# Edge tiles that belong to one node tile each, in a two-layer graph network

## The reference, cut to what matters

```python
h = relu(layernorm(x));  hh = (h @ W.T).reshape(N, 4, 32)
a_src, a_dst = (hh * att_src).sum(-1), (hh * att_dst).sum(-1)
alpha = leaky_relu(a_src[src] + a_dst[dst], 0.2)
ex = exp(alpha - segment_max(alpha, dst)[dst])
w = ex / segment_sum(ex, dst)[dst]
x = x + segment_sum(hh[src] * w[:, :, None], dst) + bias
h = relu(layernorm(x))
m = relu(concat(h[src], h[dst], edge_attr) @ W1 + b1) @ W2 + b2
x = x + segment_sum(m, src)
```

## Time and profile before

| | us |
|---|---|
| median of 3 runs (7310.71 to 7337.83) | 7331.83 |
| span of the profiled execution, first to last instruction | 7415.3 |
| start, up to the first batch's sums | 178 |
| attention stage, 62 batches | 2970 |
| node stage | 97 |
| target stage, 62 batches | 2800 |
| source stage and output | 1370 |

### The profile page before, as it was taken

One profiled execution on the slowest core, in us unless ns is written; L12 is line 12 of the kernel. 1 busy time (PEld: TensorE's weight loads), 2 busy tenths in 40 slices (PEclk: granted clock), 3 DMA queues, 4 the chain that ended last, 5 costly groups with the idle time before them and its releaser, 6 DMA issues.

```text
span 7415.3 us, 158159 instructions
## 1 busy us (share of the span) xinstructions
PE 5830.3 (79%) x34498; PEld 4483.9 (60%) x34499; DVE 4072.9 (55%) x14406; ACT 2876.8 (39%) x8241; POOL 3921.0 (53%) x3713
## 2 busy tenths in 40 slices
PE   4777776777777767767788788778778779999999
PEld 3666665666566656645555555555555557777777
DVE  5555555555555555653333333343333358888887
ACT  3333333333333333322222222222222247777776
POOL 4555555555555555465555555555555555555543
PEclk6777777766767776779988888898888889999999
DMA  3311111111111111366666666666666669999998
GB/s 89 123 37 37 37 37 37 37 36 37 37 37 37 37 37 37 102 191 194 193 194 190 195 189 194 190 192 190 197 185 188 191 178 214 214 214 213 214 212 195
DMA packets 860289, 993.31 MB, mean 134 GB/s; under 512 B 307992, under 2 KB 663224, under 8 KB 859774
## 3 DMA queue, kind: packets, MB, share of 16 engines
q1 hardware_dynamic: 662494, 608.23, 31.0%
q0 software_dynamic: 190592, 378.22, 19.3%
q10 hardware_dynamic: 6816, 3.38, 0.2%
HBM read 726.65 MB, written 262.76 MB: 133 GB/s over the span
## 4 chain that ended last, share of the span: by engine, by line
PE 66%; another core or an unknown queue 12%; issue 10%; DVE 6%; DVEq 3%; ACT 2%; DMA 1%; ACTq 0%; POOL 0%; SPq 0%; POOLq 0%
PE bank L1527 16%; PE bank L1686 10%; PE bank L1621 9%; PE bank L1619 8%; PE bank L1676 6%; PE bank L1455 4%; PE bank L1465 4%; PE bank L1609 2%; DVEq L246 2%; ACT arena L623 1%; PE bank L1574 1%; PE bank L1667 1%; DVE arena L1193 1%; DVE arena L1238 1%
## 5 line engine op out<-in xcount | busy, mean ns | idle before, releaser
L494 POOL DMA_INDIRECT arena<-h_tab,arena x1612 | 1592.0, 988 | 1474.2 <-PE bank L1527 857.6
L544 POOL DMA_INDIRECT xr<-arena x1612 | 1585.0, 983 | 1233.2 <-ACT arena L705 731.7
L1527 PE MATMUL bank<-arena 128*128 128x136 f32 x6448 | 1625.0, 392 | 77.6 <-DVE arena L1044 6.2
L1621 PE MATMUL bank<-arena 128*128 128x256 f32 x3224 | 1111.9, 430 | 486.4 <-DVE arena L1254 359.7
L705 ACT ACTIVATE arena<-bank 128x256 f32<-128x256 f32 x1612 | 598.0, 384 | 2141.4 <-PE bank L1621 1246.7
L1527 PEld LDWEIGHTS bank<-arena 128*128 128x128 f32 x6448 | 1227.4, 263 | 149.2 <-issue 108.6
L623 ACT ACTIVATE arena<-bank 128x256 bf16<-128x256 bf16 x1612 | 614.4, 383 | 1803.5 <-PE bank L1455 1108.3
L1044 DVE TENSOR_TENSOR arena<-arena,bank 128x272 f32 x1612 | 699.9, 434 | 1006.3 <-PE bank L1527 689.8
L1619 PE MATMUL bank<-arena 128*128 128x256 f32 x3224 | 1113.0, 430 | 9.9 <-DVE arena L1238 9.9
L1621 PEld LDWEIGHTS bank<-arena 128*128 128x128 f32 x3224 | 655.6, 212 | 707.7 <-DVE arena L1254 450.2
L558 POOL DMA_INDIRECT arena<-p_tab,arena x428 | 667.9, 1561 | 659.6 <-DMA arena<-p_tab,arena 439.6
(11 more groups left out here) (253 smaller groups left out, 7124.2 us busy)
## 6 DMA issues: line engine op xcount, KB each, us to landing
arena<-xr SPq DMA_DIRECT2D x428, 516.0 KB
arena<-q_tab SPq DMA_DIRECT2D x1612, 128.0 KB
arena<-in_edge_attr SPq DMA_DIRECT2D x61, 832.0 KB
arena<-rel_tab SPq DMA_DIRECT2D x124, 224.0 KB
arena<-h_tab,arena POOLq DMA_INDIRECT x1612
xr<-arena POOLq DMA_INDIRECT x1612
arena<-rel_tab SPq DMA_DIRECT2D x124, 192.0 KB
xr<-arena SPq DMA_DIRECT2D x26, 516.0 KB
```

Of the source, the lines that this page charges most:

```text
L494: pool.indirect_dma_start(G[:, q, t, :], None, h_tab, bass.IndirectOffsetOnAxis(ap=idx[:, q, t:t + 1], axis=0)).then_inc(sem(f"gath{q}"), 16)
L544: pool.indirect_dma_start(xr, bass.IndirectOffsetOnAxis(ap=pos[:, q, t:t + 1], axis=0), Rb[:, t, :], None).then_inc(sem(f"scat{m}"), 16)
L1527: last = pe.matmul(PSB[3 + t % 2][:, k * H * MW:(k + 1) * H * MW], OH[:, (t + 2 * q) % 4, k * P:(k + 1) * P], flat(msg[:, t, :, :]), start ...
L1621: pe.matmul(o, EAT[:, (t // 2 + q) % 2, :], w1z[:, t % 2, :], start=False, stop=True).then_inc(sem("main_done"), 1)
```

## The change

An edge tile now belongs to one node tile only. The row of 128 edges that straddles a border is taken twice, once for each node tile, with the edges of the other node tile masked (source and target -1). So T = 13 x 128 = 1664 tiles (1612 rows, at most 48 of them twice, the rest empty), and NB = 64 batches.

- One-hot, its transpose and its float form are 128 wide; there is one transpose, one expand matmul, one aggregation matmul (136 columns) and one add of 136 columns for a tile.
- At the start, ScalarE loads the last target of each row of edges (4 bytes each); DVE and TensorE count rows below each border, and from that the bin and the row of each tile (whole_rows, tile_rows). The bins go through DRAM (bt_tab) into bin_row. GpSimd gathers the rows of targets and sources with 27 indirect DMAs. DVE masks them (target_rows, source_rows) and makes the flags before they are transposed (flag_rows); ScalarE moves the flags out of PSUM. The tables d0_tab and col_tab and their loads go.
- In the target stage the window of q_tab starts at 128 times the bin. The edge features of a batch are loaded tile by tile: 26 DMAs of 32 KB in the place of one of 832 KB, each with its row (tile number less bin) worked out in registers, after a second load of 26 bins.
- Masked edges go to rows of xr of their own (dump is 26 wide).

```diff
-BT = 26
-NG = T // TG
+BT = 26
+NG = 13
+T = NG * P
 NB = T // BT
...
-        G, OHb = X([2, BT, GW]), X([2, BT, 2 * P], BF16)
+        G, OHb = X([2, BT, GW]), X([2, BT, P], BF16)
...
+            def load_ea(b, q, last=False):
+                regs = bins(ENG.SP, b, BT)
+                whole = TAIL - (NB - 1) * BT if last else BT
+                for t in range(whole):
+                    row = nc.s_assert_within(b * BT + t - regs[t], 0, WHOLE - 1, ...)
+                    sp.dma_start(EAb[:, q, t, :], ea[bass.ds(row * P, P), :]).then_inc(sem(f"ea_in{q}"), 16)
...
-                    regs = nc.values_load_multi_w_load_instructions(d0row[0:1, bass.ds(b * RB, BT)], engines=[ENG.SP], ...)
+                regs = bins(ENG.SP, b, BT)
...
-                        sp.dma_start(Qw[:, t, :], q_tab[bass.ds(regs[t], P), :]).then_inc(sem(f"rows_in{m}"), 16)
+                        sp.dma_start(Qw[:, t, :], q_tab[bass.ds(regs[t] * P, P), :]).then_inc(sem(f"rows_in{m}"), 16)
...
-            pool.wait_ge(sem("e_in"), 16 * 15)
-            for a in range(3):
-                M.tensor_copy(rF[:, a, :], rI[:, a, :]).then_inc(sem("rF_ready"), 1)
+            pool.wait_ge(sem("tiles_ready"), 1)
+            for v, into, n, landed in ((dst, rD, NG + 1, "rD_in"), (src, rS, NG, "rS_in")):
+                for j in range(n):
+                    pool.indirect_dma_start(into[0:p, j, :], None, wholes(v), bass.IndirectOffsetOnAxis(ap=trowI[0:p, j:j + 1], axis=0)).then_inc(sem(landed), 16)
...
+            def target_rows():
+                dve.wait_ge(sem("rD_in"), 16 * (NG + 1))
+                link(V.tensor_tensor(r3, rD, tbase.unsqueeze(2).to_broadcast([P, NG + 1, P]), ALU.subtract))
+                link(V.tensor_scalar(valid, rel, 0.0, None, ALU.is_ge))
+                link(V.scalar_tensor_tensor(valid, rel, float(P), valid, ALU.is_lt, ALU.mult))
+                link(V.scalar_tensor_tensor(rel, rel, 1.0, valid, ALU.add, ALU.mult))
...
-                A.activation(ohT[:, t % 2, :], PSB[t % 2][:].bitcast(BF16)[:, 0:2 * P], ACT.Copy)
+                A.activation(ohT[:, t % 2, :], PSB[t % 2][:].bitcast(BF16)[:, 0:P], ACT.Copy)
...
-                a = flat(acc[:, bass.ds(regs[t], 2), :])
-                V.tensor_tensor(a, a, PSB[3 + t % 2][:, 0:2 * H * MW], ALU.add)
+                a = flat(acc[:, bass.ds(regs[t], 1), :])
+                V.tensor_tensor(a, a, PSB[3 + t % 2][:, 0:H * MW], ALU.add)
...
-                for k in range(2):
-                    last = pe.transpose(PSB[t % 2][:].bitcast(BF16)[:, k * P:(k + 1) * P], OHb[:, s, t, k * P:(k + 1) * P], identb)
+                pe.transpose(PSB[t % 2][:].bitcast(BF16)[:, 0:P], OHb[:, s, t, :], identb)
...
-                for k in range(2):
-                    last = pe.matmul(ab_ps[half][:, j, :, :]..., ohT[:, t % 2, k * P:(k + 1) * P], flat(aT3[:, bass.ds(regs[t] + k, 1), :, :]), start=(k == 0), stop=(k == 1))
+                pe.matmul(ab_ps[half][:, j, :, :]..., ohT[:, t % 2, :], flat(aT3[:, bass.ds(regs[t], 1), :, :]), start=True, stop=True)
...
-                    for k in range(2):
-                        last = pe.matmul(PSB[3 + t % 2][:, k * H * MW:(k + 1) * H * MW], OH[:, (t + 2 * q) % 4, k * P:(k + 1) * P], flat(msg[:, t, :, :]), start=True, stop=True)
+                    pe.matmul(PSB[3 + t % 2][:, 0:H * MW], OH[:, (t + 2 * q) % 4, :], flat(msg[:, t, :, :]), start=True, stop=True)
```

More of the change, by code:

```diff
@@ L231, in flat @@
             return v.rearrange(f"p {d} -> p ({d})") if len(v.shape) > 2 else v
+        LISTS = [(j, min(j + 4, NG)) for j in range(0, NG, 4)]
+        FLAGS = [(0, 7), (7, NG)]
+        turned_tiles = lambda v: v[:, 0:T].rearrange("e (p j) -> e j p", j=NG)
         PIECES = [(m * BT // 4, (m + 1) * BT // 4) for m in range(4)]
@@ L360, in load_windows @@
                 B = b * BT
-                regs = nc.values_load_multi_w_load_instructions(
-                    d0row[0:1, bass.ds(b * RB, BT)], engines=[ENG.SP], min_val=0, max_val=NPAD,
-                    skip_runtime_bounds_check_because="the first target node of a tile")[1]
+                regs = bins(ENG.SP, b, BT)
                 for m, (lo, hi) in enumerate(PIECES):
@@ L816, in _, with whole_rows @@
             V.memset(srcE[:, T:], -1.0)
-            V.memset(dE[:, T:], -1.0)
-            V.memset(nE[:, T:], -1.0)
+            V.memset(dBE[:, T:], -1.0)
+            for v in (lastE, s1E, s2E):
+                V.memset(v[:, T:], 0.0)
+            def whole_rows():
+                dve.wait_ge(sem("w_in"), 80)
+                dve.wait_ge(sem("pads"), 4)
+                link(V.tensor_tensor(below, lastV.unsqueeze(1).to_broadcast([P, NT, NG]),
+                                     edge.unsqueeze(2).to_broadcast([P, NT, NG]), ALU.is_lt))
+                V.tensor_reduce(whole, below, AX.X, ALU.add).then_inc(sem("wx_ready"), 1)
@@ L855, in _ @@
                     if n == 1:
-                        dve.wait_ge(sem("w_in"), 48)
+                        dve.wait_ge(sem("w_in"), 80)
                         V.tensor_scalar(attb[:, 0:H], hm, att[:, 0:1], None, ALU.mult)
                         V.tensor_scalar(attb[:, H:], hm, att[:, 1:2], None, ALU.mult).then_inc(sem("wx_ready"), 1)
+                    if n == 2:
+                        tile_rows()
                     if n == 5:
-                        dve.wait_ge(sem("rF_ready"), 3)
-                        for g in range(NG):
-                            V.tensor_scalar(relB[:, g, :], rF[:, 1, g * P:(g + 1) * P], rF[:, 1, g * P:g * P + 1], None,
-                                            ALU.subtract).then_inc(sem("rF_ready"), 1)
+                        target_rows()
                     if n == 6:
-                        lists((0,))
+                        source_rows()
                     scaled(n - 1)
@@ L1135, in _ @@
                 hot(1, 1, t, True)
[L1136 removed]
+            empty_bins()
             logits(0, 0, 0)
@@ L1437, in _ @@
                     project(c - 1)
-            lists((1, 2))
-            project(NCH - 1)
-            lists(range(3, NG))
+                else:
+                    pe.wait_ge(sem("wx_ready"), 1)
+                    pe.matmul(PSB[3][:, 0:NT], ones, whole, start=True, stop=True).then_inc(sem("wx_ps"), 1)
+            pe.wait_ge(sem("row_made"), 1)
+            lists(srcR, 0)
+            project(NCH - 1)
+            lists(rel, 1)
+            pe.wait_ge(sem("hx_ready"), NCH)
+            for a, v in enumerate((lastR, firstR, finalR)):
+                pe.wait_ge(sem("row_made"), a + 2)
+                flags(v, a)
             pe.wait_ge(sem("hx_used"), NCH)
```

301 lines of the change are left out of this document (161 added, 140 removed).

## The result

The change made the kernel slower: 7465.9 us (median of 4 runs, 7462.9 to 7491.6) against 7334.8 us (4 runs) on the same chip, ratio 1.0192 with a 95% interval of 1.0168 to 1.0216. The forecast was 6744 us, with 0.04 for slower.

What follows compares the result with a forecast made beforehand. PE was taken as the longest member of the attention stage's ring of waits. Attention -696, target +90, start +10 and node +8 sum to -588 from 7415.3: span 6827, less 83.5 to the median, 6744 us; range 6558 to 7020.

Steps and rivals of the forecast that it cites:

- no batch can be shorter than 32.8: Attention stage: POOL's 26 gathers, starting every 1.26 us, set a floor of 32.8 us for a batch.
- rival 1: Attention stage: POOL's floor is reached, 32.8 to 34.5 us for a batch; at 33, 6558 us in all; chance 0.20.
- I take 36, between PE's and DVE's readings: Attention batch: PE's busy plus idle time gives 32.4 us, DVE's busy time plus waits 37.7; 36 taken, bounds 32.8 and 42.4.
- The term of 8 us: Attention stage: DVE's 8.0 us of waits in a batch that the profile calls remote or issue, assumed to stay.
- the ring: Attention stage: each batch is a ring of waits through PE, ACT, DVE and POOL, PE the longest member; 48.8 us.
- Rival 2: Attention stage: PE drops to its half clock and the stalls stay, 40 us for a batch, 6992 us in all; chance 0.20.
- Rival 4: Attention stage: order of waits holds the batch at 48.8 us, 7538 us in all; slower above 45.5; chance 0.05.
- So the move is hidden, with 5 us to spare: Target stage: SP's added transfers delay the next batch's first piece, but it still comes before it is needed at 45 us.
- SP's sum of 34 to 43, likely 38 us: Target stage: SP's time for a batch with 25 more DMAs, about 0.6 us each, and a second load of bins.
- rival 3: Target stage: SP becomes the bound at 1 us for an edge-feature DMA, batch 50 us, 7051 us in all; chance 0.08.
- The three signs that I had named for being wrong: POOL still waits long for PE each batch; window loads end DVE's or PE's target-stage waits; start grows over 25 us.
- Start, +10 forecast: Start: 27 gathers take 34 to 39 us, first h_tab gather 10 us later than 75.8; +10 us, bounds 0 and +25.

Runs made afterwards that it cites:

- e12: Changed kernel with a small GpSimd fill after each attention gather, gathers 1.44 us apart and more, late-signal chip: 7566.1 us, 1.0216 of before.
- e11: Kernel before the change, without GpSimd's gathers from the third batch on, late-signal chip: 6448.9 us, attention batch 33.3 us.
- e15: Changed kernel without GpSimd's gathers from the third batch on, late-signal chip: 6707.0 us, attention batch 30.7 us.
- e4: Changed kernel, a batch's edge features in one transfer, no second load of bins, chip without late signals: 5897.4 us, 1.0146 of before.
- e9: Changed kernel, edge features in 13 two-tile transfers from static rows, no second load of bins, late-signal chip: 7346.2 us, target batch 45.0 us.
- e8: Changed kernel, 26 edge-feature transfers from static rows, no second load of bins, late-signal chip: 7394.1 us, target batch 45.8 us.
- e6: Changed kernel, unedited, rerun on a chip without late signals: 6204.1 us, 1.0673 of before.
- e18: Changed kernel with a GpSimd fill after each target-stage scatter alone, late-signal chip: 7258.4 us, 0.9898 of before.

## Why the prediction was wrong

The miss is 722 us: attention 502, target 136, start 28, the other stages -4; the last 60 are the step from span to median, taken as -83.5 us, where this profiled execution is 23 us above its median.

**Attention, -696 forecast, -194 measured.** The costs of VectorE's and ScalarE's instructions held. So did "no batch can be shorter than 32.8", and the order of the bounds: on a prompt chip POOL leads with 32.9 us for a batch, as in rival 1, but there the kernel before is near the floor already, at 34.3, and with two more batches the stage is 4 us shorter. The step that failed is "How near does the batch come to 32.8? ... I take 36, between PE's and DVE's readings". Both readings came out too low. DVE's had 23.0 us busy, 5.7 of waits for the aggregation, 8.0 "remote or issue" and 1 of small ones; measured are 23.1, 7.2, 11.8 and 2.0. PE's had 19 busy and 13.4 idle; measured are 27.7 and 16.4. The term of 8 us "that no releaser explains", kept constant, was the sign. On the chip of the result a good part of the idle time is signals held back by the gathers, whose number per tile doesn't change: the same program without them, or on a prompt chip, takes 30.7 or 32.9 us a batch, at or under the lower bound. Why the late signals cover more of the shorter batch isn't shown. Longer runs of gathers without a wait fit the traces of before and after, but e12 has no such runs and as many late signals.

The earlier trace rows held part of the evidence: copies 10 us apart beside free-running gathers. The earlier trace rows held less than it seems. I read its 0.84 us for a tile as proof that the ring is short; against 1.88 us it lacks both the gathers and the work ahead, and e11, without the gathers alone, takes 1.28.

**Rival 2** came nearest. Its clock (0.51 measured, 0.5 assumed) and its 27 busy us (27.7) were right; the idle time was 16.4 us, not 13.4. The Trainium skill ("TensorE: Matmul & The Clock Gate", Why this matters for your kernels) has gaps between bursts return the array to its half clock; the trace agrees for the change on this chip, 0.51 for a whole stage with TensorE busy 63% of it where it was 0.71 with 73%. It isn't the whole of it: without gathers the clock is 0.51 after the change and 0.89 before, with TensorE busy 85% and 83% (e15, e11). Nor is the clock what holds the batch: at 0.50 it is 32.9 us on a prompt chip. What rival 2 lacked was the growth of the stalls.

**Rival 4**, "the batch doesn't follow PE's work", had the sign's side right and its mechanism half right: break-even at 45.5 us assumed the other stages as forecast. The batch came to 44.1, and the target stage turned the sign: without its 136 us over the forecast the two medians would be level.

**Target, +90 forecast, +226 measured.** The step that failed is "So the move is hidden, with 5 us to spare". SP's sum of 34 to 43, likely 38 us held on a prompt chip, 38.3 at the 0.6 us assumed. On the result's chip the same work takes SP 47.2 us, 0.71 to 0.73 for an edge-feature transfer and 0.80 for a window, and it hardly ever waits. That is the mechanism of rival 3, reached below its own threshold of 0.8 us for a transfer, since the windows became dearer too. The three signs that I had named for being wrong all came: POOL waits 6.8 us of an attention batch for PE (310.0 of 2000 us), the window loads ended VectorE's waits for 166 us of 2100, and the start grew by 38 us. The cover was less than it looked as well. The 45.2 us that "PE sets" are 33.2 on a prompt chip, where no signal is late; that late signals make the difference is read from the traces (12.3 us of a target batch before the change), for no run left the scatters out. The Trainium skill ("DMA: Bandwidth & Descriptors", Rules for kernel authors) warns against many small transfers; e4 agrees with the direction, 33.2 us a batch against 38.2, though it drops a load of bins as well; so does e9, 45.0 against e8's 45.8. The 52 us a batch that I had estimated from the same page's fixed cost were not seen: SP paid 0.60 to 0.73 us for each.

**Start, +10 forecast, +38 measured** (+23 on a prompt chip). The 27 gathers of rows were to take 1.26 to 1.43 us each. From the view of their line:

```profile
L487 POOL DMA_INDIRECT arena<-in_dst,arena x14: 948/1690/3227, 23.9 to 51.0; - x14
L487 POOL DMA_INDIRECT arena<-in_src,arena x13: 952/2457/2670, 53.9 to 79.5; - x13
...
  DVE arena L873: 16.5, 1
  DVE arena L865: 11.9, 1
```

They last 58 us instead of 34 to 39, and VectorE stands 11.9 and 16.5 us for them (L865, L873) with the last chunks of the projection behind. The first gather of h_tab starts at 114.0 us, not 86. What stretched those gathers wasn't tried; it isn't the late signals, for they are as long in e6. **Node stage:** -2 instead of +8. **Source stage:** +6, forecast 0.

**What stays open.** Shown is that GpSimd's gathers hold back other engines' signals on some chips, with half the bytes or half the rows as well, and that spreading the scatters makes SP issue faster there. By what path, and in what the two kinds of chip differ, no run here tells; nor what pace would be free of it. At 1.44 us between gathers the late signals are as many, at the source stage's 3.1 us there are none, and nothing was tried between.

## What to carry to other kernels

Before counting on shorter work, ask the trace which waits have no named releaser, and where in it the suspected engine is silent: a stage with and one without GpSimd's indirect DMAs, side by side, give their price. If one engine already has a floor close to the batch (here 34.3 against 32.8), narrower work elsewhere is worth only the difference. A queue's time is hidden only as long as the stage is as long as it was: work out what the stage takes when its stalls go, and hold the queue against that. And ask the trace whether the issuing engine itself still waits: here it stood 819 of 2100 us before the change and 10 after.

## What the runs showed of the hardware

- The same program took 5811 to 5813 us on two chips and 7301 to 7409 us on the others. Of the 1605 us between the two profiles of the kernel before, 864 stand in the attention and 742 in the target stage, where GpSimd issues an indirect DMA for every tile; the source stage takes 1370 to 1398 us in the profiles of both kernels on both kinds.
- On the late chips signals between the other engines came up to 6 us late in the attention stage, and VectorE's independent instructions 1.40 us apart, while GpSimd itself kept its 1.26 us. On a prompt chip the same 26 instructions took 4.37 us beside the same gathers.
- An indirect DMA of the attention stage costs GpSimd 0.95 us with 128 rows and 0.91 with 64, at full or half the bytes; the source stage's, which add to their destination, 1.55.
- 8138 matmuls of the attention stage kept TensorE busy as long as 14163 had, 1676 against 1734 us, as the granted clock went from 0.88 to 0.50.
- SP pays 0.60 us for a transfer whose row it works out in registers on a prompt chip, 0.71 to 0.73 on the chip of the result, and 0.63 on a late chip when a fill of GpSimd follows each scatter (e18).
